# Where the product with silu(z) is made: from the scan stage's VectorE to the routing stage's GpSimd

## What is computed

```python
z = layernorm(x)                                  # (4, 1024, 1024)
for each step t:                                  # selective scan, state (e, n), 16 values of n
    state = state * exp(delta[t] * A) + (delta[t] * u[t]) * B[t]
    y[t]  = einsum('ben,bn->be', state, C[t])
y = y + D[None, :, None] * u
y = y * silu(z)
x = x + tanh(g_xattn) * swapaxes(y, 1, 2)
h = layernorm(x)
x = x + tanh(g_ffn) * (routed_experts(h) + shared_expert(h))
```

## Time and profile before

| | us |
|---|---|
| median of three timed runs | 4159.72 |
| the profiled execution | 4151.87 |
| its span, first to last instruction | 4149.8 |
| stage 1, about | 0 to 492 |
| stage 2, about | 492 to 1745 |
| stage 3, about | 1745 to 2430 |
| stages 4 and 5, about | 2430 to 4150 |

### The profile page before, as it was taken

One profiled execution on the slowest core, in us unless ns is written; L12 is line 12 of the kernel. 1 busy time (PEld: TensorE's weight loads), 2 busy tenths in 40 slices (PEclk: granted clock), 3 DMA queues, 4 the chain that ended last, 5 costly groups with the idle time before them and its releaser, 6 DMA issues. The chain is left out here.

```text
span 4149.8 us, 59457 instructions
## 1 busy us (share of the span) xinstructions
PE 3843.5 (93%) x21088; PEld 3146.5 (76%) x21088; DVE 3046.5 (73%) x3711; ACT 2147.3 (52%) x2256; POOL 1721.3 (41%) x977
## 2 busy tenths in 40 slices
PE   8898588898898898799999989999999999999999
PEld 3444478788788788678888868888888888788887
DVE  7888789999999999877777745555555555455555
ACT  3777689898899898722222234444444444200000
POOL 0233189999999999823333310000000000122222
PEclk9999599999999999899999989999999999999999
DMA  6677843643643643455555646767766666677543
GB/s 234 243 283 251 294 142 105 182 147 104 187 138 109 182 137 118 138 185 177 185 182 184 223 167 235 242 235 241 242 233 235 229 235 232 226 278 264 196 164 117
DMA packets 328294, 819.57 MB, mean 197 GB/s; under 512 B 65920, under 2 KB 109696, under 8 KB 318784
## 3 DMA queue, kind: packets, MB, share of 16 engines
q1 hardware_dynamic: 296240, 750.13, 52.9%
q0 software_dynamic: 31744, 67.23, 5.5%
q10 hardware_dynamic: 144, 0.00, 0.0%
HBM read 603.38 MB, written 245.27 MB: 205 GB/s over the span
## 5 line engine op out<-in xcount | busy, mean ns | idle before, releaser
L1095 POOL TENSOR_TENSOR h<-h,c 128x1024 f32<-128x1024 f32 x512 | 1205.3, 2410 | 38.1 <-DVE h L1078 34.6
L1078 DVE TENSOR_TENSOR_SCAN h<-da,dbu 128x1024 f32<-128x1024 f32 x512 | 1134.8, 2273 | 68.2 <-ACT dbu L1041 39.3
L1048 ACT ACTIVATE da<-dl,ad 128x1024 f32<-128x1024 f32 x512 | 588.4, 1149 | 82.5 <-DVE h L1078 69.3
L1126 PE MATMUL psy<-ident,h 128*128 128x128 f32 x4096 | 562.5, 281 | 44.2 <-POOL h L1095 24.7
L1041 ACT ACTIVATE dbu<-psb 128x1024 f32<-128x1024 f32 x510 | 520.8, 1021 | 72.2 <-PE psb L1116 64.1
L2032 DVE TENSOR_TENSOR wsp<-arena,wsp 128x2048 fp32r<-128x2048 f32 x198 | 447.7, 2289 | 100.4 <-ACT wsp L1984 100.4
L1126 PEld LDWEIGHTS psy<-ident,h 128*128 128x128 f32 x4096 | 447.9, 143 | 77.7 <-POOL h L1095 50.0
L1870 POOL DMA_INDIRECT xg<-scratch_xn,ids x64 | 63.3, 990 | 1032.0 <-PE psT L1888 1010.7
L1984 ACT ACTIVATE wsp<-arena 128x2048 fp32r<-128x2048 f32 x198 | 370.2, 1909 | 23.8 <-DMA arena<-in_w 23.4
L1116 PE MATMUL psb<-m,du_taps 128*128 128x128 f32 x2048 | 288.7, 288 | 63.6 <-ACT dbu L1041 63.4
L1116 PEld LDWEIGHTS psb<-m,du_taps 128*128 128x128 f32 x2048 | 251.5, 193 | 101.1 <-ACT dbu L1041 96.1
(11 more groups left out here) (215 smaller groups left out, 7911.9 us busy)
## 6 DMA issues: line engine op xcount, KB each, us to landing
arena<-in_w SPq DMA_DIRECT2D x192, 1024.0 KB, 6.9
du_taps<-scratch_duT SPq DMA_DIRECT2D x496, 128.0 KB, 2.9
c<-scratch_c SPq DMA_DIRECT2D x64, 512.0 KB, 8.2
scratch_xT<-xT_s SPq DMA_DIRECT2D x32, 1024.0 KB, 4.9
scratch_ob<-ob SPq DMA_DIRECT2D x64, 512.0 KB, 2.6
xT_place<-scratch_xT SPq DMA_DIRECT2D x32, 1024.0 KB, 6.3
scratch_duT<-duT SPq DMA_DIRECT2D x52, 512.0 KB, 4.0
xz<-in_x SPq DMA_DIRECT2D x32, 512.0 KB, 5.6
```

The source lines that it names most:

```text
L1048: act.activation(da[k % 2][:, :], dl[:, i % 2, :], ACT.Exp, scale=ad[:, i % 2, n:n + 1]).then_inc(s_da, 1)
L1078: dve.tensor_tensor_scan(h[:, k % HR, :], da[k % 2][:, :], dbu[:, (k // GN) % 2, k % GN, :], 0.0, ALU.mult, ALU.add).then_inc(s_scan, 1)
L1095: pool.tensor_tensor(h[:, k % HR, :], h[:, k % HR, :], c[:, n, :], ALU.mult).then_inc(s_hc, 1)
L1126: mm = pe.matmul(psy[:, t, :], h[:, k % HR, t * P:(t + 1) * P], ident[:], is_transpose=True, start=(n == 0 and t % 4 == 0), stop=(n == NST ...
```

## The change

The scan stage no longer multiplies with silu(z). ACT copies `psy` into `aux` with the factor tanh(g) (`sum_out`), behind the exp of unit n = 3 of the next tile; `gate_tile` and `load_silu` are gone. The first stage stores silu(z) in the layout of the tokens (`sz`, as `gated`), in pieces of 512 B. The routing stage loads a third tile, `sz`, for each tile of tokens, and POOL does a product and then the sum. x goes into a part of the raw weights' room (`raw[:, 1]`), so SP waits for two more split weights before it starts its loop (`s_wlo` 4), and for the last sum before it loads the first expert (`s_add`). For tiles 0 and 1 `gated` and `sz` are what is loaded ahead; x for them goes into `ac`, loaded at the stage's start after the last `gated` tile has been stored.

```diff
--- before.py
+++ after.py
@@ -337,7 +337,8 @@
 
             def store_gate(k):
                 sp.wait_ge(s_szev, 2 * k + 2)
-                sp.dma_start(dr["szT"][k].rearrange("p t c -> p (t c)"), xz[:, k % ZR, :]).then_inc(s_szst[k % ZR], 16)
+                sp.dma_start(dr["sz"][k // ET].rearrange("(t p) (e c) -> e p t c", p=P, c=P)[k % ET],
+                             xz[:, k % ZR, :].rearrange("p (t c) -> p t c", c=P)).then_inc(s_szst[k % ZR], 16)
 
             def store_du(q):
                 for part, ready in ((0, s_duhi), (1, s_dulo)):
@@ -872,7 +873,7 @@
         CP = NC // PARTS
         HR = 4
         AHEAD, BEHIND = 3, 6
-        GATED, SKIPPED = 1, 6
+        GATED, SKIPPED = 3, 6
         GATED_AT = 8
         skip = sb("skip", [P, P])
         gate = sb("gate2", [P, 1])
@@ -904,7 +905,6 @@
         s_cl = [sem(f"p2_c_loaded{n}") for n in range(NST)]
         s_ld = [sem(f"p2_delta_loaded{i}") for i in range(2)]
         s_ut = sem("p2_u_loaded")
-        s_szl = sem("p2_silu_loaded")
         s_gst = sem("p2_gated_stored")
         s_mm = sem("p2_input_multiplied")
         s_ev = sem("p2_input_copied")
@@ -958,10 +958,6 @@
                 after(sp, s_gst, i * 16)
                 sp.dma_start(ut, dr["u"][i]).then_inc(s_ut, 16)
 
-            def load_silu(i):
-                sp.wait_ge(s_skip, i + 1)
-                sp.dma_start(aux[:], dr["szT"][i]).then_inc(s_szl, 16)
-
             def store(i):
                 sp.wait_ge(s_gated, i + 1)
                 sp.dma_start(dr["gated"][i // ET].rearrange("(t p) (e c) -> e p t c", p=P, c=P)[i % ET], aux[:])\
@@ -981,7 +977,7 @@
                 sp.wait_ge(s_mm, SETS)
                 sp.wait_ge(s_gst, 16 * ET)
                 for t in range(2):
-                    for i, src_ in enumerate((dr["gated"], io["x"])):
+                    for i, src_ in enumerate((dr["gated"], dr["sz"])):
                         w0 = 2 * KH * HB + (2 * i + t) * H
                         sp.dma_start(arena[:, w0:w0 + H], src_.rearrange("b (t p) h -> (b t) p h", p=P)[t]).then_inc(early["x"][t], 16)
 
@@ -1018,7 +1014,6 @@
                 for r in range(PARTS):
                     if not final:
                         load_du(i + 1, r)
-                load_silu(i)
                 if final:
                     first_weights()
                     first_tokens()
@@ -1041,11 +1036,21 @@
                 act.activation(dbu[:, g % 2].rearrange("p n (t c) -> p n t c", c=NC)[:, :, :, r * CP:(r + 1) * CP],
                                product_bank(k).rearrange("p c t n -> p n t c"), ACT.Copy).then_inc(s_ev, 1)
 
+            def sum_out(i):
+
+                if i == 0:
+                    act.wait_ge(s_gate, 1)
+                act.wait_ge(s_skip, i + 1)
+                act.wait_ge(s_ys, i * NST + NST)
+                act.activation(aux[:], psy[:], ACT.Copy, scale=gate[:, 0:1]).then_inc(s_gated, 1)
+
             def unit(i, n, k):
                 if n == 0:
                     act.wait_ge(s_ld[i % 2], (i // 2) * 32 + 32)
                 after(act, s_scan, k - 1)
                 act.activation(da[k % 2][:, :], dl[:, i % 2, :], ACT.Exp, scale=ad[:, i % 2, n:n + 1]).then_inc(s_da, 1)
+                if n == GATED and i:
+                    sum_out(i - 1)
                 copy_input(k + AHEAD)
                 if k == GATED_AT:
                     act.wait_ge(s_c, 16)
@@ -1058,18 +1063,10 @@
             for k in range(AHEAD):
                 copy_input(k)
             units(unit)
+            sum_out(NU - 1)
 
         @block.vector
         def _(dve):
-            def gate_tile(i):
-
-                if i == 0:
-                    dve.wait_ge(s_gate, 1)
-                dve.wait_ge(s_szl, i * 16 + 16)
-                dve.wait_ge(s_ys, i * NST + NST)
-                dve.scalar_tensor_tensor(out=aux[:], in0=psy[:], scalar=gate[:, 0:1], in1=aux[:],
-                                         op0=ALU.mult, op1=ALU.mult).then_inc(s_gated, 1)
-
             def unit(i, n, k):
                 dve.wait_ge(s_da, k + 1)
                 dve.wait_ge(s_ev, (k // GN) * GN + GN)
@@ -1077,12 +1074,9 @@
                 after(dve, s_ys, k - HR + 1)
                 dve.tensor_tensor_scan(h[:, k % HR, :], da[k % 2][:, :], dbu[:, (k // GN) % 2, k % GN, :], 0.0, ALU.mult,
                                        ALU.add).then_inc(s_scan, 1)
-                if n == GATED and i:
-                    gate_tile(i - 1)
 
             dve.wait_ge(early["du_last"], 32)
             units(unit)
-            gate_tile(NU - 1)
 
         @block.gpsimd
         def _(pool):
@@ -1201,7 +1195,8 @@
             w4, ws = sb("w4", [P, TOPK]), sb("ws", [P, 2])
             pos, over, sf = sb("pos", [P, TOPK]), sb("over", [P, TOPK]), sb("sf", [P, TOPK])
             si = sb("si", [P, 2, TOPK], I32)
-            xin = rest[:, 2 * H:4 * H].rearrange("p (r h) -> p r h", r=2)
+            sz = rest[:, 2 * H:4 * H].rearrange("p (r h) -> p r h", r=2)
+            xin = raw[:, 1, 0:2 * H].rearrange("p (r h) -> p r h", r=2)
         else:
             y = raw.rearrange("p r (k h) -> p r k h", h=H)
             si = sb("si", [P, 2, TOPK], I32)
...
@@ -1254,6 +1251,10 @@
 
         @block.sync
         def _(sp):
+            if route:
+                sp.wait_ge(early["gated"], 16)
+                for par in range(2):
+                    sp.dma_start(ac[:, par, :], x0[par]).then_inc(s_x[par], 16)
             consts = [(gate[:], io["g_f"].partition_broadcast(P))]
             if route:
                 consts += [(tri[:], io["tri"]), (iota[:], io["iota"].partition_broadcast(P)),
@@ -1262,12 +1263,11 @@
                            (gw[:], io["gate_w"].rearrange("(k p) e -> p k e", p=P))]
             for dst, src in consts:
                 sp.dma_start(dst, src).then_inc(s_c, 16)
-            if route:
-                sp.wait_ge(early["gated"], 16)
 
             def load(t, par):
                 if route:
                     sp.dma_start(xt[:, par, :], gated[t]).then_inc(s_x[par], 16)
+                    sp.dma_start(sz[:, par, :], silu[t]).then_inc(s_x[par], 16)
                     sp.dma_start(xin[:, par, :], x0[t]).then_inc(s_x[par], 16)
                 else:
                     sp.dma_start(xT[:, par].bitcast(F32), dr["xT"][t]).then_inc(s_x[par], 16)
@@ -1300,6 +1300,7 @@
             def first_expert():
 
                 sp.wait_ge(s_wlo, 6)
+                sp.wait_ge(s_add, TT)
                 for m, src in enumerate((io["w1"], io["w3"])):
                     for half in range(2):
                         sp.dma_start(raw[:, m, halves[half]].rearrange("p (k f) -> p k f", k=KH // 2),
@@ -1335,6 +1336,7 @@
 
             if route:
                 store_x1(0, 0)
+                sp.wait_ge(s_wlo, 4)
             turns(sp, TT // 2, pair, last=True)
             store(TT - 2, 0)
             store(TT - 1, 1)
@@ -1349,8 +1351,13 @@
                     if isinstance(j, int) and j == 0:
                         pool.wait_ge(early["x"][par], 32)
                     else:
-                        pool.wait_ge(s_x[par], j * 32)
-                    pool.tensor_tensor(xt[:, par, :], xt[:, par, :], xin[:, par, :], ALU.add).then_inc(s_add, 1)
+                        pool.wait_ge(s_x[par], j * 48 + 16)
+                    pool.tensor_tensor(xt[:, par, :], xt[:, par, :], sz[:, par, :], ALU.mult).then_inc(s_pr, 1)
+                    first = isinstance(j, int) and j == 0
+                    if first:
+                        pool.wait_ge(s_x[par], 16)
+                    pool.wait_ge(s_pr, j * 2 + par + 1)
+                    pool.tensor_tensor(xt[:, par, :], xt[:, par, :], (ac if first else xin)[:, par, :], ALU.add).then_inc(s_add, 1)
 
                 add_x(0, 0)
                 pool.memset(ones[:], 1.0)
@@ -2076,7 +2083,7 @@
     assert FS == 2 * HB
     dt = lambda name, shape, t=F32: nc.dram_tensor(name, shape, t, kind="Internal").ap()
     dr = {k: dt("scratch_" + k, s) for k, s in dict(
-        a=(ET, P, NST + 1), x1=(TT, P, H), gated=(B, L, H), u=(B * ET, P, L), dl=(B * ET, P, L), szT=(B * ET, P, ET, P),
+        a=(ET, P, NST + 1), x1=(TT, P, H), gated=(B, L, H), u=(B * ET, P, L), dl=(B * ET, P, L), sz=(B, L, H),
         c=(B, NST, L), xn=(NT, H), acc=(TT, P, H), ob=(NE * CAP, H)).items()}
     dr["duT"] = dt("scratch_duT", (B * ET, 2, TB, NC, P))
     dr["bT"] = dt("scratch_bT", (B, 2, 2, TB * SKEW))
```

More of the change, by code:

```diff
@@ L1236, in shared_pass @@
             gated = dr["gated"].rearrange("b (t p) h -> (b t) p h", p=P)
+            silu = dr["sz"].rearrange("b (t p) h -> (b t) p h", p=P)
+            s_pr = sem("gated")
             x0 = io["x"].rearrange("b (t p) h -> (b t) p h", p=P)
```

## The result

The changed kernel took 4175.31 us (median of 10 runs, 4170.60 to 4180.38), the kernel before on the same chip 4154.07 (10 runs): a ratio of 1.0053, 95% interval 1.0043 to 1.0062, so 21 us more. The forecast was 4225, the range 4172 to 4276. The sign and the range held; the forecast rise of 71 us was more than three times too large.

What follows compares the result with a forecast made beforehand. POOL was taken to pace the scan and PE the routing, with DVE's loop 0.7 us short of PE's. Terms 1 - 5 + 10 + 54 + 9 = +69 us gave 4221 to 4229, forecast 4225, range 4172 to 4276.

Steps and rivals of the forecast that it cites:

- Extra stall: 2.5 us, bounds 2.2 ... and 2.97: Routing loop, choose: DVE stands still again behind POOL's second instruction, 2.5 us more in each iteration.
- The slack of 0.7 us: Routing loop: DVE's loop takes 19.6 us against PE's 20.29, so 0.7 us of added stall is absorbed per iteration.
- my 54 us: Routing loop: 30 iterations, each 1.8 us longer after slack, +54 us, bounds +45 and +69.
- PE's clock, +9: Routing loop: PE at half speed after waits costs about 2 us in five tiles of 30, +9 us, bounds 0 and +60.
- Routing start, +10 (6 to 12): Start of routing: the sum waits for x, loaded after the last store, so the norm comes later; +10 us.
- The branch named in the text: Start of routing: if the last store lands after 3 us instead of 6.9, the delay is 4 us less.
- Scan, -5: Scan stage, DVE: the gating goes but POOL mostly hides it, -5 us, bounds -34.6 and 0.
- Stage 1, +1: First stage: silu(z) stores in 512 B pieces lengthen SP's waits before loads of x; +1 us, bounds 0 and +5.
- ScalarE's copy, 0: Scan stage: 32 new copies of 1.117 us fit ACT's idleness, 0; if not, up to 35 us in all.
- The low ends of the terms: Whole kernel: the terms at low ends, +45, 0, +6, -10 and 0, give +41 us.
- the forecast's own range: Whole kernel: 4190 to 4262 us for the forecast case alone, before widening for rivals.
- Rival 2: Routing loop, choose: the second POOL instruction costs DVE nothing; +6, up to +15, about 4165 us; chance 0.13.

Runs made afterwards that it cites:

- The doses: Kernel before with four, later two, idle bn_stats of 512 columns added on VectorE in choose: 4179.52 and 4156.69 us.
- experiment 1: Changed kernel without GpSimd's product, so the output lacks silu(z): 4150.72 us, ratio to before 1.0001.
- experiment 9: Changed kernel with ScalarE's scan copy made twice, in unit 2, or in unit 4 instead of 3: 4244.06, 4230.37 and 4273.24 us.
- experiment 8: Changed kernel with a ring of its own for the gated tile, earlier loads, and the product beside x_rest, multiply and statistics: 4155.54 us.
- experiment 7: Changed kernel with GpSimd's product made half an iteration earlier, ahead of the scatters in program order, the sum left in place: 4194.35 us.
- experiment 6: Changed kernel with GpSimd's product and sum held back until the first half of VectorE's x_rest is written: 4205.26 us.
- experiment 5: Changed kernel with a third full-size GpSimd instruction, an idle product, ahead of the product in each routing tile: 4227.55 us.

## Why the prediction was right in direction and wrong in size

- *The step that failed is the term of each iteration, "Extra stall: 2.5 us, bounds 2.2 ... and 2.97".* Between the iterations shown E grew by 1.1 us, and by 1.3 in the median of the loop: half of it and outside my bounds. The two stalls add up to (2.40 - 0.17) + (2.07 - 0.28) = 4.02 us over the bare instructions; before, it was 2.97 - 0.17 = 2.80. The second GpSimd instruction did hold VectorE out, but VectorE gained in two places, of which I had counted the first at 0.2 to 0.4 us and the second not at all. Between the two and under the second, which took 2.55 us, it got 0.69 us of choose done (L1662, then L1666, a reduction, which isn't held). And the first stall is 0.57 shorter: in the kernel before the stall began 0.53 us ahead of GpSimd's start as the profile has it; after, VectorE was in FIND_INDEX8 then, and its stall began with GpSimd. The pair also starts 4.0 us after h_rest, not the 3 that I took; my own rows give 3.5.
- *The slack of 0.7 us: right.* The doses confirm it. It was read from the iteration with the longest E, 10.77; in the others it was up to 0.4 more.
- *PE's other waits: missed, small.* Logits follow psG after 5.91 us instead of 5.69, as the weight load for psR waits 0.4 us for ow_s in an iteration. With 0.1 more to h_rest, the loop reads 5.91 + 3.18 + 11.85 + 0.05 = 20.99 against 21.00 seen. The average iteration is 20.97, so +0.68 instead of +1.8: 28 x 0.68 = 19 of my 54 us.
- *PE's clock, +9: 0.* It stayed at 1.00 through the loop, from 1815 to 2420 us.
- *Routing start, +10 (6 to 12): +6.3.* The branch named in the text held: the store landed after 3 us, "4 us less". The expected wait behind the second GpSimd instruction came, at 2.1 us.
- *Scan, -5: -2.1 in the pair of profiles, -4.5 between the means of seven and four (experiment 1).* The term held.
- *Stage 1, +1: +2.5.* It can't be told from scatter: VectorE's first scan began at 500.8 to 504.6 us in four profiles with the old stores and at 500.1 to 504.0 in ten with the new.
- *ScalarE's copy, 0: right,* and by less than 1.1 us (experiment 9). PE's wait for psy at a tile's start grew from 0.6 to 1.2 us, the 0.6 that I had read.
- *A sum.* The low ends of the terms give +41, which is 4193 on the profiled execution, not the 4190 of the forecast's own range.
- *Rival 2 ("the second instruction costs VectorE nothing"), +6 and up to +15, was nearer to the time than the forecast,* but its mechanism is not what happened: the second cost VectorE half its length. The truth lay between two cases that I had kept apart.
- *The Trainium skill's rule* (SBUF — State Buffer, section "Who interferes with whom") holds in kind: instructions with two SBUF inputs stood, and so did a cast and tensor_scalars of 4 and 32 columns; reductions, maxima, bn_stats and those with an input in PSUM ran. I took it for a price of the instruction's whole length. The price hangs on which of VectorE's instructions come due in that window: E grew over 10.77 by 1.1 us here, by nothing in experiment 8 and by 1.3 or 2.3 in experiment 7.

## What to carry to other kernels

Before you price a GpSimd instruction that locks VectorE out, lay VectorE's own order beside it and count only what is held there; then ask where the next iteration puts it, since a loop can swing between two phases. The remedy here was a place, not a size: a product moved beside instructions that aren't held cost the loop nothing, while halving product and sum left the time where it was, and moving it took a buffer of its own so that its load could go earlier. For work slipped in between on an engine with slack, look up who waits for its end: a copy of 1.1 us was free in one unit and cost 1.7 and 3.1 us a tile in its neighbours. And look at the clock that PE was granted before you put such a cost down to the wait alone.

## What the runs showed of the hardware that I had not expected

- VectorE's stall can begin 0.5 us ahead of GpSimd's start in the profile: L1650 took 2.97 us beside a sum of 2.40.
- A cast of 128x4 and a two-scalar instruction of 128x4 took 2.40 and 3.11 us when held, where they need 0.17 and 0.29; reductions and bn_stats weren't held at all.
- Loops swing: 21.94 and 20.28 us in turn, 21.67 and 20.28 in halves.
- GpSimd's sum took 2.55 us, not 2.40, where VectorE's L1662 began within 0.01 us of it. That the two hinder each other there is my reading and not shown.
- PE fell to 1.2 GHz for about 3 us in every second or third iteration of experiment 6, where it waited 0.7 us in each; with waits of 1.3 us in each settled iteration of experiment 5 it stayed at 2.4. With 2.2 us in the early ones, and 3.3 us at the tile starts of the copy in unit 4, it fell nearly every time.
